# One signal for each corner of an item, in place of one for each unit, in a deformable convolution

## The chip, the cores and the metric

The kernel runs on one core of one Trainium2 chip. The metric is the time of one execution on the device in microseconds (us). The kernel before was timed three times.

## The reference

The input x has 4 images of 128 channels and 48 x 48 pixels, in float32. Two layers are computed, each added to its input:

```python
x = x + deform_conv_bn_relu(group_norm(x))   # layer 0
x = x + conv3x3(group_norm(x)) + bias        # layer 1

# layer 0, for each pixel and each of the 9 taps:
om   = conv3x3(x, w_offset) + b_offset       # 27 channels: dy, dx, mask
cols = mask * (corner(y0, x0)     * (1-ly)*(1-lx) + corner(y0, x0+1)     * (1-ly)*lx
             + corner(y0+1, x0)   * ly*(1-lx)     + corner(y0+1, x0+1)   * ly*lx)
out  = einsum('bckhw,ock->bohw', cols, wk) + b_conv
```

The four corners are gathered at places that depend on the data, and `out` then goes through a batch norm and a relu.

## The kernel before, in words

The 4 x 2304 pixels are cut into 24 **chunks** of 384 pixels (3 tiles of 128). A **unit** is one tap for one tile: 128 pixels on the partitions, 4 corners of 128 channels each in the free direction of tile `g`. A chunk has 9 taps x 3 tiles = 27 units, grouped into 9 **items** of 3 units (one tap, three tiles). The first and the last chunk order their units by tile; the last chunk has 11 items, and its two last ones have 2 and 1 units.

Layer 0 is a pipeline over items, written out by hand on five queues; semaphores tie them together:

- POOL issues one indirect DMA for each unit (line 299), 27 for a chunk, which fetches all four corners from a table in DRAM into `g`. It starts on a chunk when the chunk's indices are ready (`idx_ready`), and each group of three waits until the item of the chunk before that used its place in `g` is summed (`lerped`, line 297). `g` has one place for each unit, so chunk c+1 is fetched while the later items of chunk c are still summed.
- ACT multiplies the first corner by its weight, one instruction for each unit, into PSUM tile `PA` (line 557; semaphore `scaled`). It copies transposed items out of PSUM (`cols`, line 538; waits for `turned` and `conved`, signals `copied`), and copies a finished chunk out (`o`, line 548).
- DVE adds the products of corners 1, 2 and 3 (line 770): for an item of three units, nine instructions, corner by corner and in each corner unit by unit. Corners 1 and 2 write back into `PA`, corner 3 writes `acc`. Each one signals `lerped`. An instruction of corner 2 or 3 waits for the instruction of the corner before on the same unit. After item 4 of a chunk DVE computes the indices of the next chunk (lines 708 to 744; `idx` is line 717), and after item 2 the statistics of the chunk before (line 754).
- PE transposes `acc` (line 403; waits for `lerped`, signals `turned`), multiplies by the weights (line 392; signals `conved`), and spreads the offset convolution of the next chunk over items 0, 1 and 2 (line 352).
- The order on ACT is: scale item k, copy item k-1, and for k = 1 copy out the chunk before. So ACT can't scale item 2 of a chunk before it has copied item 0 and the chunk before.

After the 24 chunks come the batch norm, the relu and layer 1, which the change doesn't touch.

Of the kernel before, what the change touches and what calls it, by code (L numbers as in the profile page):

```python
# [6 lines left out]
ALU = mybir.AluOpType  # L7
ACT = mybir.ActivationFunctionType

P = 128  # L10
B, H, W = 4, 48, 48
HW = H * W
TAPS = 9
PW = W + 2
TILES = 3
# [20 lines left out]
LAST_SETS = ((0, 1, 2), (3, 4, 5), (6, 7), (8,))  # L36

TILE_ROWS = 3
LERP = 3


def items(c):

    if c not in BY_TILE:
        return [[(k, t) for t in range(TILES)] for k in range(TAPS)]
    return [[(k, t) for k in taps] for t in range(TILES) for taps in (LAST_SETS if (c, t) == (ALL - 1, TILES - 1) else TAP_SETS)]


def first_item(c):
    return sum(len(items(i)) for i in range(c))  # L50


def units_before(c, i):

    return c * TAPS * TILES + sum(len(units) for units in items(c)[:i])


def last_use(c, unit):
# [32 lines left out]
def build(nc, x_d, tab_d, woff_d, wconv_d, w1_d, boff_d, par_d, grid_d, out_d):  # L91

    with ExitStack() as ctx:
# [12 lines left out]
        g = sb("g", [P, TAPS, TILES, 4, P])  # L106

        mixed = g[:].rearrange("p k t q c -> p (k t q c)")[:, 0:MIX * PW * HALF].rearrange("p (m r w) -> p m r w", m=MIX, w=HALF)
        acc = sb("acc", [P, 3, TILES, P])
# [156 lines left out]
        @block.gpsimd  # L266
        def _(pl):
            xn4 = xn[:].rearrange("p (b r) w -> p b r w", b=B)
            pl.memset(wz[:], 0.0).then_inc(consts, 1)
            pl.memset(eps[:], EPS).then_inc(consts, 1)  # L270
            pl.memset(last_stats[:, 0:1], float(B * HW - 2 * P)).then_inc(consts, 1)
            pl.memset(gshift[:], 0.0).then_inc(consts, 1)
            pl.memset(gavg[:], 1.0 / GROUP).then_inc(consts, 1)
            pl.memset(ident[:], 0.0).then_inc(consts, 1)
            gv = gavg[:].rearrange("p (a b) -> p a b", b=GROUP)
            pl.wait_ge(consts, 5)
            pl.affine_select(out=gv, in_=gv, compare_op=ALU.is_ge, fill=0.0, base=0,
                             pattern=[[-GROUP, P // GROUP], [0, GROUP]], channel_multiplier=1).then_inc(consts, 1)
            pl.wait_ge(consts, 7)
            pl.affine_select(out=gv, in_=gv, compare_op=ALU.is_ge, fill=0.0, base=GROUP - 1,  # L280
                             pattern=[[GROUP, P // GROUP], [0, GROUP]], channel_multiplier=-1).then_inc(consts, 1)
            pl.affine_select(out=ident[:], in_=ident[:], compare_op=ALU.not_equal, fill=1.0, base=0,
                             pattern=[[-1, P]], channel_multiplier=1).then_inc(consts, 1)
            pl.memset(xn4[:, :, 0:PW:PW - 1, :], 0.0).then_inc(consts, 1)
            pl.memset(xn4[:, :, 1:1 + H, 0:PW:PW - 1], 0.0).then_inc(consts, 1)

            for c in range(ALL):
                pl.wait_ge(idx_ready, 1 if c == 0 else part_count(c))
                for i, units in enumerate(items(c)):
                    if c == 0 and i == len(TAP_SETS):  # L290
                        pl.wait_ge(idx_ready, 2)
                    if c:

                        used = max(last_use(c - 1, unit) for unit in units)
                        if i < len(items(c - 1)):
                            used = max(used, i)
                        pl.wait_ge(lerped, units_before(c - 1, used + 1) * LERP)
                    for k, t in units:
                        pl.indirect_dma_start(  # L299
                            out=g[:, k, t].rearrange("p q c -> p (q c)"), out_offset=None, in_=tab_d,  # L300
                            in_offset=bass.IndirectOffsetOnAxis(ap=idx[:, c % 2, t, k:k + 1], axis=0),
                        ).then_inc(gathered[i], 16)

            def add(b):
                for j in range(0, BANDS, 2):
                    pl.wait_ge(relued, b * BANDS + (BAND_ORDER.index(j) + 1))
                    add_band(pl, b, j).then_inc(added, 1)

            def mix_band(b, h):
                pl.wait_ge(normed, b * BANDS + (h + 1))  # L310
                if b:

                    pl.wait_ge(conv1, MIX * ((b - 1) * BANDS + min(h + 2, BANDS)))
                for m in range(MIX):
                    mix(pl, b, h, m).then_inc(mixed_ready, 1)

            add(0)
            for b in range(B - 1):
                mix_band(b, 1)
                mix_band(b, 2)  # L320
                add(b + 1)
                mix_band(b, 3)
                mix_band(b + 1, 0)
            for h in range(1, BANDS):
                mix_band(B - 1, h)

        @block.tensor
        def _(pe):
# [67 lines left out]
            def turn_item(c, i):  # L396
                units = items(c)[i]
                s = first_item(c) + i
                pe.wait_ge(lerped, units_before(c, i + 1) * LERP)
                if s > 1:  # L400
                    pe.wait_ge(copied, s - 1)
                for n in range(len(units)):
                    last = nc.tensor.transpose(TP[s % 2][:, n * P:(n + 1) * P], acc[:, s % 3, n, :], ident[:])  # L403
                last.then_inc(turned, 1)
# [87 lines left out]
        def _(act):  # L492
# [57 lines left out]
            def scale_item(c, i):  # L550
                s = first_item(c) + i
                act.wait_ge(gathered[i], landed(c, i))
                if s > 1:

                    act.wait_ge(lerped, (units_before(c, i - 1) if i else units_before(c - 1, len(items(c - 1)) - 1)) * LERP)
                for n, (k, t) in enumerate(items(c)[i]):
                    nc.scalar.activation(PA[s % 2][:, n * P:(n + 1) * P], g[:, k, t, 0, :], ACT.Copy,  # L557
                                         scale=wt[:, c % 2, 0, t, k:k + 1]).then_inc(scaled, 1)

            for i in (1, 3):  # L560
                act.dma_start(x[:, X0[i] * CP:X0[i + 1] * CP], x_d[:, 0, X0[i] * CP:X0[i + 1] * CP]).then_inc(x0_in[i], 16)
# [73 lines left out]
        def _(dve):  # L635
# [120 lines left out]
            def lerp_item(c, i):  # L756
                units = items(c)[i]
                s = first_item(c) + i
                done = units_before(c, i)
                dve.wait_ge(gathered[i], landed(c, i))  # L760

                dve.wait_ge(scaled, done + len(units))
                for q in range(1, 4):
                    for n, (k, t) in enumerate(units):
                        if q > 1:
                            dve.wait_ge(lerped, done * LERP + (q - 2) * len(units) + n + 1)
                        if q == 3 and n == 0 and s > 2:
                            dve.wait_ge(turned, s - 2)
                        a = PA[s % 2][:, n * P:(n + 1) * P]
                        nc.vector.scalar_tensor_tensor(acc[:, s % 3, n, :] if q == 3 else a, g[:, k, t, q, :],  # L770
                                                       wt[:, c % 2, q, t, k:k + 1], a, ALU.mult, ALU.add).then_inc(lerped, 1)

            statistics(0)
            deviation(0)
# [151 lines left out]
```

## Time and profile before

| | us |
|---|---|
| median of 3 runs | 1330.88 |
| lowest and highest | 1327.02 and 1339.39 |
| the profiled execution, its own time | 1331.31 |
| its span (first to last instruction) | 1329.6 |
| DVE busy | 687.7 (52% of the span) |
| POOL busy | 669.0 (50%) |
| PE busy (matmuls) | 783.9 (59%) |
| ACT busy | 369.8 (28%) |

Busy time is summed over each engine's instructions; waits and signals are not in it. No engine is busy for much more than half of the span, so the time is a matter of what waits for what. "Remote" or "issue" as the end of an idle time means that the profile names no instruction that ended just then.

### The profile page before, as it was taken

Reading aid. Unit: us, or ns where it says so; the run is one execution under the profiler, and the core shown is the slowest. Engines: PE = TensorE matmul, PEld = TensorE weight load, DVE = VectorE, ACT = ScalarE, POOL = GpSimd, SP = SyncE. Lnnn points to the kernel's source line nnn. Section 1 sums busy time; section 2 is a strip of 40 time slices with the busy share of each in tenths; the row PEclk is TensorE's granted clock in tenths of the full one; section 3 lists DMA queues with packets and bytes.
Section 4 is the critical chain, followed back from the end, with each engine's and each line's share of the span. In section 5 each row is a group of like instructions: output and inputs, shape, how many; then the busy total and the mean of one; then the engine's idle time right before and its main releaser. Section 6 shows DMA issues by size and latency. Waiting matters only on the chain.

```text
span 1329.6 us, 10583 instructions
## 1 busy us (share of the span) xinstructions
PE 783.9 (59%) x2380; PEld 376.8 (28%) x2380; DVE 687.7 (52%) x2662; ACT 369.8 (28%) x1026; POOL 669.0 (50%) x731
## 2 busy tenths in 40 slices
PE   7463646655555544656555544656555556555999
PEld 4232222222122222222122122222122122135777
DVE  4337446446447446446437536536436436465664
ACT  3213224223213214313213214313213213234320
POOL 4374374373473474374464465364364364361743
PEclk8665766767766767767776767767777677666999
DMA  7364464363473374373474364374364364360011
GB/s 282 118 183 126 118 199 117 111 201 108 119 206 108 116 209 117 104 208 108 116 204 114 117 197 129 99 199 120 104 203 123 107 198 127 104 176 22 37 53 54
DMA packets 55971, 181.50 MB, mean 137 GB/s; under 512 B 10980, under 2 KB 11492, under 8 KB 55524
## 3 DMA queue, kind: packets, MB, share of 16 engines
q0 software_dynamic: 51840, 169.91, 44.4%
q1 hardware_dynamic: 3780, 10.32, 2.1%
q10 hardware_dynamic: 288, 0.59, 0.1%
q14 instruction: 43, 0.35, 0.1%
q8 instruction: 20, 0.33, 0.1%
HBM read 176.06 MB, written 4.72 MB: 136 GB/s over the span
## 4 chain that ended last, share of the span: by engine, by line
another core or an unknown queue 27%; PE 22%; issue 21%; DVE 19%; ACT 10%; DMA 1%; POOL 1%; ACTq 0%; DVEq 0%; SPq 0%
DVE PA L770 10%; ACT PA L557 8%; PE OMT L352 5%; PE CO L392 5%; DVE acc L770 5%; PE TP L403 4%; PE TP L477 2%; PE PA L477 2%; PE CO L477 2%; ACT cols L538 1%; PE OMT L477 1%; PE VU L477 1%; DMA g<-corner_table,idx 1%; DVE bst L688 1%
## 5 line engine op out<-in xcount | busy, mean ns | idle before, releaser
L299 POOL DMA_INDIRECT g<-corner_table,idx x648 | 612.7, 946 | 581.4 <-DVE idx L717 366.2
L770 DVE SCALAR_TENSOR_TENSOR PA<-g,wt,PA 128x128 f32<-128x128 f32 x1296 | 358.0, 349 | 496.4 <-ACT PA L557 300.0
L403 PE MATMUL TP<-ident,acc 128*128 128x128 f32 x648 | 157.4, 367 | 398.4 <-DVE acc L770 216.8
L392 PE MATMUL CO<-cols,wcs 128*128 128x384 f32 (+1 forms) x504 | 266.1, 637 | 130.0 <-issue 100.1
L538 ACT ACTIVATE cols<-TP 128x384 f32<-128x384 f32 (+1 forms) x217 | 104.9, 484 | 736.8 <-remote 364.3
L403 PEld LDWEIGHTS TP<-ident,acc 128*128 128x128 f32 x648 | 90.2, 178 | 533.7 <-DVE acc L770 280.7
L352 PE MATMUL OMT<-xn,woff 128*27 128x384 f32 (+2 forms) x450 | 231.0, 671 | 1.2 <-ACT mask L519 0.7
L770 DVE SCALAR_TENSOR_TENSOR acc<-g,wt,PA 128x128 f32<-128x128 f32 x648 | 191.5, 342 | 63.5 <-DVE acc L770 36.5
L557 ACT ACTIVATE PA<-g,wt 128x128 f32<-128x128 f32 x648 | 203.3, 358 | 9.8 <-DMA g<-corner_table,idx 8.9
L392 PEld LDWEIGHTS CO<-cols,wcs 128*128 128x128 f32 x504 | 109.8, 279 | 160.1 <-issue 113.6
L352 PEld LDWEIGHTS OMT<-xn,woff 128*27 128x27 f32 x450 | 55.7, 138 | 177.7 <-issue 174.9
L245 POOL TENSOR_TENSOR g<-xn 128x288 f32<-128x288 f32 (+1 forms) x60 | 41.9, 731 | 34.3 <-ACT xn L623 33.2
L378 PE MATMUL CO<-vt,ut 9*128 9x384 f32 (+1 forms) x56 | 32.2, 666 | 0.0
L237 POOL TENSOR_TENSOR x<-x,o 128x576 f32<-128x576 f32 x8 | 11.5, 1454 | 23.1 <-ACT o L617 23.0
L530 ACT ACTIVATE vt<-VU 9x384 f32<-9x384 f32 x24 | 11.5, 478 | 32.4 <-issue 15.1
L367 PE MATMUL VU<-ident,vsum 128*9 128x128 f32 x72 | 17.7, 374 | 2.6 <-issue 2.6
L523 ACT ACTIVATE std<-OMT,eps 128x1 f32<-128x1 f32 x5 | 1.3, 261 | 59.4 <-PE OMT L335 59.4
L519 ACT ACTIVATE mask<-OMT 128x27 f32<-128x27 f32 (+2 forms) x25 | 4.8, 192 | 46.0 <-DVE pos L709 43.2
L548 ACT ACTIVATE o<-CO,params 128x384 f32<-128x384 f32 x23 | 13.2, 575 | 13.2 <-remote 12.8
L477 PE MATMUL OMT<-g,w 128*128 128x288 f32 x48 | 14.6, 444 | 2.2 <-DVE g L245 2.2
L496 ACT ACTIVATE xn<-x,gshift,gscale 128x1872 f32<-128x1872 f32 (+3 forms) x9 | 10.8, 1236 | 17.8 <-DVE gshift L682 11.1
L367 PEld LDWEIGHTS VU<-ident,vsum 128*9 128x9 f32 x72 | 9.1, 128 | 20.1 <-issue 18.6
(119 smaller groups left out, 495.7 us busy)
## 6 DMA issues: line engine op xcount, KB each, us to landing
g<-corner_table,idx POOLq DMA_INDIRECT x648
out_dram<-x SPq DMA_DIRECT2D x16, 288.0 KB, 2.1
x<-x_dram SPq DMA_DIRECT2D x3, 1152.0 KB, 8.1
wconv<-wconv_dram SPq DMA_DIRECT2D x1, 576.0 KB, 5.2
w<-w_dram SPq DMA_DIRECT2D x1, 576.0 KB
x<-x_dram ACTq DMA_DIRECT2D x1, 384.0 KB, 5.0
x<-x_dram SPq DMA_DIRECT2D x1, 384.0 KB, 4.7
x<-x_dram ACTq DMA_DIRECT2D x1, 192.0 KB, 3.5
```

Of the source, the lines that this page charges most:

```text
L245: return eng.tensor_tensor(mixed[:, m, first:first + rows, :], p, q, op)
L299: pl.indirect_dma_start(out=g[:, k, t].rearrange("p q c -> p (q c)"), out_offset=None, in_=tab_d, in_offset=bass.IndirectOffsetOnAxis(ap=i ...
L352: last = nc.tensor.matmul(OM[:, first * W:(first + rows) * W], woff[:, k, :], xn[:, row + k // 3:row + k // 3 + rows, k % 3:k % 3 + W], st ...
L367: last = nc.tensor.transpose(VT[:, t * P:(t + 1) * P], vsum[:, t, :], ident[:])
L378: nc.tensor.matmul(co_bank(c, t)[:, lo:hi], ut[:, c // CHUNKS % 2, :], vt[:, lo:hi], start=True, stop=False)
L392: last = nc.tensor.matmul(co_bank(c, t)[:, t * P:t * P + size], wcs[:, c // CHUNKS % 2, k, :], cols[:, s % 2, n * P:n * P + size], start=F ...
L403: last = nc.tensor.transpose(TP[s % 2][:, n * P:(n + 1) * P], acc[:, s % 3, n, :], ident[:])
L477: last = nc.tensor.matmul(MX[h % 2][m][:, 0:HB], w, mixed[:, m, r:r + BR, :], start=(ky == 0), stop=(ky == 2))
L538: nc.scalar.activation(cols[:, s % 2, 0:size], TP[s % 2][:, 0:size], ACT.Copy).then_inc(copied, 1)
L557: nc.scalar.activation(PA[s % 2][:, n * P:(n + 1) * P], g[:, k, t, 0, :], ACT.Copy, scale=wt[:, c % 2, 0, t, k:k + 1]).then_inc(scaled, 1)
L688: nc.vector.bn_stats(bst[:, j, :], x[:, b * HW + j * CP:b * HW + (j + 1) * CP]).then_inc(stats_in, 1)
L770: nc.vector.scalar_tensor_tensor(acc[:, s % 3, n, :] if q == 3 else a, g[:, k, t, q, :], wt[:, c % 2, q, t, k:k + 1], a, ALU.mult, ALU.add ...
```

## The change

DVE and ACT do the same instructions in the same order. What changes is which of them signal, and what is waited for:

- ACT's three scalings of an item signal `scaled` once, from the last one, in place of three times.
- DVE's three sums of one corner signal `lerped` once, from the last one: 3 signals for an item in place of 9.
- The wait of corner 2 and corner 3 stands once, ahead of the first unit, and is for the whole corner before. Before, each unit waited for its own unit alone.
- The counts that POOL, PE and ACT wait for are rewritten to match. They stand for the same moments: a whole item done.

```diff
--- before.py
+++ after.py
@@ -36,6 +36,7 @@
 LAST_SETS = ((0, 1, 2), (3, 4, 5), (6, 7), (8,))
 
 TILE_ROWS = 3
+
 LERP = 3
 
 
@@ -48,11 +49,6 @@
 
 def first_item(c):
     return sum(len(items(i)) for i in range(c))
-
-
-def units_before(c, i):
-
-    return c * TAPS * TILES + sum(len(units) for units in items(c)[:i])
 
 
 def last_use(c, unit):
@@ -294,7 +290,7 @@
                         used = max(last_use(c - 1, unit) for unit in units)
                         if i < len(items(c - 1)):
                             used = max(used, i)
-                        pl.wait_ge(lerped, units_before(c - 1, used + 1) * LERP)
+                        pl.wait_ge(lerped, (first_item(c - 1) + used + 1) * LERP)
                     for k, t in units:
                         pl.indirect_dma_start(
                             out=g[:, k, t].rearrange("p q c -> p (q c)"), out_offset=None, in_=tab_d,
@@ -396,7 +392,7 @@
             def turn_item(c, i):
                 units = items(c)[i]
                 s = first_item(c) + i
-                pe.wait_ge(lerped, units_before(c, i + 1) * LERP)
+                pe.wait_ge(lerped, (s + 1) * LERP)
                 if s > 1:
                     pe.wait_ge(copied, s - 1)
                 for n in range(len(units)):
@@ -552,10 +548,10 @@
                 act.wait_ge(gathered[i], landed(c, i))
                 if s > 1:
 
-                    act.wait_ge(lerped, (units_before(c, i - 1) if i else units_before(c - 1, len(items(c - 1)) - 1)) * LERP)
+                    act.wait_ge(lerped, (s - 1) * LERP)
                 for n, (k, t) in enumerate(items(c)[i]):
-                    nc.scalar.activation(PA[s % 2][:, n * P:(n + 1) * P], g[:, k, t, 0, :], ACT.Copy,
-                                         scale=wt[:, c % 2, 0, t, k:k + 1]).then_inc(scaled, 1)
+                    last = nc.scalar.activation(PA[s % 2][:, n * P:(n + 1) * P], g[:, k, t, 0, :], ACT.Copy, scale=wt[:, c % 2, 0, t, k:k + 1])
+                last.then_inc(scaled, 1)
 
             for i in (1, 3):
                 act.dma_start(x[:, X0[i] * CP:X0[i + 1] * CP], x_d[:, 0, X0[i] * CP:X0[i + 1] * CP]).then_inc(x0_in[i], 16)
@@ -756,19 +752,19 @@
             def lerp_item(c, i):
                 units = items(c)[i]
                 s = first_item(c) + i
-                done = units_before(c, i)
                 dve.wait_ge(gathered[i], landed(c, i))
 
-                dve.wait_ge(scaled, done + len(units))
+                dve.wait_ge(scaled, s + 1)
                 for q in range(1, 4):
+                    if q > 1:
+                        dve.wait_ge(lerped, s * LERP + q - 1)
+                    if q == 3 and s > 2:
+                        dve.wait_ge(turned, s - 2)
                     for n, (k, t) in enumerate(units):
-                        if q > 1:
-                            dve.wait_ge(lerped, done * LERP + (q - 2) * len(units) + n + 1)
-                        if q == 3 and n == 0 and s > 2:
-                            dve.wait_ge(turned, s - 2)
                         a = PA[s % 2][:, n * P:(n + 1) * P]
-                        nc.vector.scalar_tensor_tensor(acc[:, s % 3, n, :] if q == 3 else a, g[:, k, t, q, :],
-                                                       wt[:, c % 2, q, t, k:k + 1], a, ALU.mult, ALU.add).then_inc(lerped, 1)
+                        last = nc.vector.scalar_tensor_tensor(acc[:, s % 3, n, :] if q == 3 else a, g[:, k, t, q, :],
+                                                              wt[:, c % 2, q, t, k:k + 1], a, ALU.mult, ALU.add)
+                    last.then_inc(lerped, 1)
 
             statistics(0)
             deviation(0)
```

On DVE in a chunk of the middle, items 3 and 4, before (the line number of the sum is 770 before and 765 after, since lines went from the file; `gathered3` is the landing of item 3's gathers):

```order
L770 SCALAR_TENSOR_TENSOR PA<-g,wt,PA 128x128 [waits scaled,gathered3]
L770 SCALAR_TENSOR_TENSOR PA<-g,wt,PA 128x128 x2
L770 SCALAR_TENSOR_TENSOR PA<-g,wt,PA 128x128 [waits lerped] x3
L770 SCALAR_TENSOR_TENSOR acc<-g,wt,PA 128x128 [waits turned,lerped]
L770 SCALAR_TENSOR_TENSOR acc<-g,wt,PA 128x128 [waits lerped] x2
L770 SCALAR_TENSOR_TENSOR PA<-g,wt,PA 128x128 [waits scaled,gathered4]
L770 SCALAR_TENSOR_TENSOR PA<-g,wt,PA 128x128 x2
L770 SCALAR_TENSOR_TENSOR PA<-g,wt,PA 128x128 [waits lerped] x3
L770 SCALAR_TENSOR_TENSOR acc<-g,wt,PA 128x128 [waits turned,lerped]
```

and now:

```order
L765 SCALAR_TENSOR_TENSOR PA<-g,wt,PA 128x128 [waits scaled,gathered3]
L765 SCALAR_TENSOR_TENSOR PA<-g,wt,PA 128x128 x2
L765 SCALAR_TENSOR_TENSOR PA<-g,wt,PA 128x128 [waits lerped]
L765 SCALAR_TENSOR_TENSOR PA<-g,wt,PA 128x128 x2
L765 SCALAR_TENSOR_TENSOR acc<-g,wt,PA 128x128 [waits turned,lerped]
L765 SCALAR_TENSOR_TENSOR acc<-g,wt,PA 128x128 x2
L765 SCALAR_TENSOR_TENSOR PA<-g,wt,PA 128x128 [waits scaled,gathered4]
L765 SCALAR_TENSOR_TENSOR PA<-g,wt,PA 128x128 x2
L765 SCALAR_TENSOR_TENSOR PA<-g,wt,PA 128x128 [waits lerped]
L765 SCALAR_TENSOR_TENSOR PA<-g,wt,PA 128x128 x2
L765 SCALAR_TENSOR_TENSOR acc<-g,wt,PA 128x128 [waits turned,lerped]
```

The order is the same. Where all three sums of corner 2 and corner 3 waited, the first one waits now, and for the last sum of the corner before, which stands directly ahead of it.

On DVE at the end of the last chunk, the items of two units and of one unit, before:

```order
L770 SCALAR_TENSOR_TENSOR PA<-g,wt,PA 128x128 [waits scaled,gathered8]
L770 SCALAR_TENSOR_TENSOR PA<-g,wt,PA 128x128
L770 SCALAR_TENSOR_TENSOR PA<-g,wt,PA 128x128 [waits lerped] x2
L770 SCALAR_TENSOR_TENSOR acc<-g,wt,PA 128x128 [waits turned,lerped]
L770 SCALAR_TENSOR_TENSOR acc<-g,wt,PA 128x128 [waits lerped]
L770 SCALAR_TENSOR_TENSOR PA<-g,wt,PA 128x128 [waits scaled,gathered9]
L770 SCALAR_TENSOR_TENSOR PA<-g,wt,PA 128x128 [waits lerped]
L770 SCALAR_TENSOR_TENSOR acc<-g,wt,PA 128x128 [waits turned,lerped]
```

and now:

```order
L765 SCALAR_TENSOR_TENSOR PA<-g,wt,PA 128x128 [waits scaled,gathered8]
L765 SCALAR_TENSOR_TENSOR PA<-g,wt,PA 128x128
L765 SCALAR_TENSOR_TENSOR PA<-g,wt,PA 128x128 [waits lerped]
L765 SCALAR_TENSOR_TENSOR PA<-g,wt,PA 128x128
L765 SCALAR_TENSOR_TENSOR acc<-g,wt,PA 128x128 [waits turned,lerped]
L765 SCALAR_TENSOR_TENSOR acc<-g,wt,PA 128x128
L765 SCALAR_TENSOR_TENSOR PA<-g,wt,PA 128x128 [waits scaled,gathered9]
L765 SCALAR_TENSOR_TENSOR PA<-g,wt,PA 128x128 [waits lerped]
L765 SCALAR_TENSOR_TENSOR acc<-g,wt,PA 128x128 [waits turned,lerped]
```

In the item of one unit nothing differs: there the wait was already for the instruction directly ahead.

## Rows read from the trace of the kernel before

**Rows 1.** Page of the kernel before, costliest groups of instructions.

```profile
L299 POOL DMA_INDIRECT g<-corner_table,idx x648 | 612.7, 946 | 581.4 <-DVE idx L717 366.2
L770 DVE SCALAR_TENSOR_TENSOR PA<-g,wt,PA 128x128 f32<-128x128 f32 x1296 | 358.0, 349 | 496.4 <-ACT PA L557 300.0
L770 DVE SCALAR_TENSOR_TENSOR acc<-g,wt,PA 128x128 f32<-128x128 f32 x648 | 191.5, 342 | 63.5 <-DVE acc L770 36.5
```

**Rows 2.** Timeline of POOL, chunks 9 to 11: start, length, and idle time before.

```profile
463.35 0.94 POOL L299 DMA_INDIRECT g<-corner_table,idx  x1 [15.29 <-DVE idx L717]
...
511.89 0.94 POOL L299 DMA_INDIRECT g<-corner_table,idx  x1 [15.14 <-DVE idx L717]
...
544.40 0.95 POOL L299 DMA_INDIRECT g<-corner_table,idx  x1 [0.30 <-issue]
...
562.69 0.94 POOL L299 DMA_INDIRECT g<-corner_table,idx  x1 [17.34 <-DVE idx L717]
```

**Rows 3.** Windows by stage of chunk 10.

```profile
core 0: us, PE busy (x) PEld busy (x) DVE busy (x) ACT busy (x) POOL busy (x), PEclk, DMA share, GB/s
511.90:529.00 17.10, 7.68 (x20) 3.69 (x18) 11.03 (x52) 7.43 (x18) 13.14 (x14) 0.53 0.67 187
529.00:547.00 18.00, 5.10 (x12) 1.75 (x12) 5.63 (x20) 2.42 (x8) 12.39 (x14) 0.66 0.73 211
...
550.00:562.70 12.70, 12.44 (x54) 5.52 (x52) 9.85 (x41) 7.18 (x20) 0.01 (x1) 0.92 0.01 2
```

**Rows 4.** Timeline of DVE, items 0 and 1 of chunk 10.

```profile
531.14 0.87 DVE L770 SCALAR_TENSOR_TENSOR PA<-g,wt,PA 128x128 f32<-128x128 f32 x3
536.46 0.35 DVE L770 SCALAR_TENSOR_TENSOR PA<-g,wt,PA 128x128 f32<-128x128 f32 x1 [4.46 <-remote]
537.86 0.35 DVE L770 SCALAR_TENSOR_TENSOR PA<-g,wt,PA 128x128 f32<-128x128 f32 x1 [1.05 <-DVE PA L770]
...
548.37 0.35 DVE L770 SCALAR_TENSOR_TENSOR PA<-g,wt,PA 128x128 f32<-128x128 f32 x1 [4.47 <-remote]
```

**Rows 5.** Timeline of all engines, chunk 1.

```profile
69.03 0.94 POOL L299 DMA_INDIRECT g<-corner_table,idx  x1 [19.26 <-DVE PA L770]
...
85.04 0.55 PE L403 MATMUL TP<-ident,acc 128*128 128x128 f32 x3
...
92.22 0.49 ACT L538 ACTIVATE cols<-TP 128x384 f32<-128x384 f32 x1 [12.24 <-remote]
...
105.52 0.58 ACT L548 ACTIVATE o<-CO,params 128x384 f32<-128x384 f32 x1 [12.81 <-remote]
...
107.01 0.49 ACT L538 ACTIVATE cols<-TP 128x384 f32<-128x384 f32 x1
107.04 1.39 DVE L770 SCALAR_TENSOR_TENSOR PA<-g,wt,PA 128x128 f32<-128x128 f32 x5 [24.55 <-ACT PA L557]
```

**Rows 6.** Timeline of POOL, ACT, DVE and PE, chunk 18.

```profile
909.95 0.94 POOL L299 DMA_INDIRECT g<-corner_table,idx  x1 [16.21 <-DVE idx L717]
...
947.92 0.49 ACT L538 ACTIVATE cols<-TP 128x384 f32<-128x384 f32 x1 [10.68 <-remote]
...
949.82 1.65 DVE L770 SCALAR_TENSOR_TENSOR PA<-g,wt,PA 128x128 f32<-128x128 f32 x6 [8.66 <-ACT PA L557]
...
954.01 0.87 PE L403 MATMUL TP<-ident,acc 128*128 128x128 f32 x3
...
956.79 1.65 DVE L770 SCALAR_TENSOR_TENSOR PA<-g,wt,PA 128x128 f32<-128x128 f32 x6 [1.78 <-ACT PA L557]
```

**Rows 7.** Timeline of DVE, items 3 and 4 of chunk 9.

```profile
506.11 1.63 DVE L770 SCALAR_TENSOR_TENSOR PA<-g,wt,PA 128x128 f32<-128x128 f32 x6
...
508.42 1.64 DVE L770 SCALAR_TENSOR_TENSOR PA<-g,wt,PA 128x128 f32<-128x128 f32 x6
```

**Rows 8.** Timeline of DVE, last item of the last chunk (one unit).

```profile
1213.12 0.74 DVE L770 SCALAR_TENSOR_TENSOR PA<-g,wt,PA 128x128 f32<-128x128 f32 x2
1213.89 0.35 DVE L770 SCALAR_TENSOR_TENSOR acc<-g,wt,PA 128x128 f32<-128x128 f32 x1
```

## Prediction

> **What bounds the kernel now.** I read the page's groups first, then POOL's timeline, then the windows of one chunk, then the waits on DVE and ACT inside it. No engine is full, but POOL shows the beat: it issues 648 gathers and sits idle 581.4 us before them, 366.2 us of that until DVE's index instruction [rows 1]. In chunk 10 the first gather starts at 511.89 and the last at 544.40, 26 steps of 1.25 us, and then POOL waits until 562.69, when the indices of chunk 11 are there [rows 2]. Chunks 1 to 10 took (562.69 - 69.03) / 10 = 49.4 us each [rows 2, 5]. So a chunk is some 34 us of issue and some 15 us from the last gather to the next indices, and all that DVE does in these 15 us is on the path.
>
> The windows show why DVE is not done by then. While gathers are issued and land, DMA moves 187 to 211 GB/s, and in the second half of that DVE is busy for 5.63 of 18 us; when they are over it is busy for 9.85 of 12.70 us [rows 3]. Between, DVE's sums stand 1.40 us apart, and once 4.46 us behind the sum before, where three sums in a row otherwise take 0.87 us [rows 4]. Signals arrive late there. A signal of PE shows it more plainly: in chunk 1 PE has transposed item 0 by 85.6 us, and ACT, which has nothing else to do, goes on at 92.22, at 105.52 and at 107.01 [rows 5]. Then all signals that were under way are there at once. This clearing comes at the same distance from the first gather: 107.01 - 69.03 = 38.0 us in chunk 1, 947.92 - 909.95 = 38.0 in chunk 18 [rows 5, 6]. In chunk 18 DVE starts item 2 at 949.82, 1.9 us after it, since ACT first copies item 0 and the finished chunk and scales item 2 [rows 6].
>
> The period is thus: 38.0 us to the clearing, 1.9 us of ACT, then items 2, 3 and 4 and the indices on DVE, 9 to 11 us.
>
> **Part 1: signals that go (6 of 9 on DVE, 2 of 3 on ACT).** They take no busy time. Where they are late they cost: 1.40 us for each on DVE in items 0 and 1 of a chunk. But does the clearing come sooner with fewer of them? Chunk 1 is the test: DVE is idle for 24.55 us before its sum at 107.04 [rows 5], so no signal of DVE's can be in the way for most of that time, and the clearing is at 38.0 us all the same as in chunk 18. PE's signals, which keep their number, are late there too. So the clearing belongs to the gathers. What items 0 and 1 gain ends in a longer wait for item 2, and I take zero. The exceptions are chunks 4, 10 and 16, where item 0 starts late and item 1 runs over the clearing: in chunk 10 DVE starts the second corner of item 1 at 548.37 [rows 4], and PE, which does its work in order, is late for item 1 and all behind it. That chunk took 562.69 - 511.89 = 50.8 us against 48.5 of chunk 9 [rows 2]. With three signals for an item instead of nine, item 0 should end some microseconds sooner. The gain is between 0 and 2.3 us; PE's and ACT's extra work in these chunks stays, so I take 1.25 us, less the price of part 2: a net -1.0 us for each, **-3 us** for the three.
>
> The Trainium skill ("VectorE: DVE Perf Modes", section "The DRAIN you can't avoid") reports eight copies in a chain taking the same time with a signal from each and from the last alone. No run here shows that yet; it would leave only the late signals as a gain.
>
> **Part 2: the wait that gets closer.** Before, the first unit of a corner waits for an instruction two places back; now for the one directly ahead. Three sums of 349 ns take 0.87 us [rows 1, 4], so they start (0.87 - 0.35) / 2 = 0.26 us apart: each starts before the one ahead has ended. With a wait for the one directly ahead this overlap is lost. The last item of the last chunk has one unit and so has this wait already: its sums start (1213.89 - 1213.12) / 2 = 0.385 us apart [rows 8]. The price is 0.385 - 0.26 = 0.125 us for each corner change, two in an item, **0.25 us for an item**. From below it is bounded by 0 (if the overlap were kept), from above by the 1.40 us of a late signal [rows 4]. After the clearing, where the path is, DMA is at rest and [rows 8] is the nearest row, so I take 0.125.
>
> How much of it is on the path:
> - Items 5 to 8, 0 and 1 run before the clearing, with idle time behind them. Zero, as long as item 1 ends before the clearing.
> - Items 2, 3 and 4 run after it. In 4 of the 22 middle chunks (3, 9, 14, 15) item 4 follows item 3 without a gap: chunk 9 has item 3 at 506.11 and item 4 at 508.42, 2.31 us, just nine sums [rows 7]. Three items count: 0.75 x 4 = 3.0 us.
> - In chunks 1 and 8 a gap of 0.17 us takes some of it: 0.58 x 2 = 1.2. In 6, 12 and 21 the gap is 0.4 to 0.5: 0.35 x 3 = 1.0. In 19 it takes all that items 2 and 3 add: 0.25.
> - In 9 more (2, 5, 7, 11, 13, 17, 18, 20, 22) item 4 waits for PE: in chunk 18 the transposes of item 2 start at 954.01, long after item 2, and item 4 at 956.79 after 1.78 us of idle time [rows 6]. What items 2 and 3 add is hidden there: 0.25 x 9 = 2.25.
> - Chunk 0 has two items on the path, 0.5. In the last chunk five items follow the clearing with two corner changes each, some of it under ACT's work: 1.1. There POOL also waits for items of chunk 22 in another order than they are summed, so that its gathers start later by what items 5 to 8 add: 1.0.
>
> Sum: 3.0 + 1.2 + 1.0 + 0.25 + 2.25 + 0.5 + 1.1 + 1.0 = 10.3, less 3 = **+7.3 us**.
>
> **Part 3: signals that are coarser.** PE, POOL and ACT waited for whole items already, and DVE for all three scalings, and the last instruction of each still signals. Zero, with nothing to hide.
>
> The profiled execution took 1331.31, 0.43 above the median. 1331.3 + 7.3 = 1338.6 against it, **1338** against the median, +0.5%.
>
> **Rivals.**
> 1. *The close wait meets late signals (slower).* Before, a sum's own signal had a quarter of a microsecond to arrive without holding anything; now none. If items 6 to 8 or 0 and 1 then pay 1.40 us at each of two corner changes, item 1 runs over the clearing in all chunks, as in chunk 10. Each of 19 chunks goes from 49.4 to 50.8: 27 us more, and the 10.3 of part 2: 1331 + 27 + 10 = **1368**. For it: the 4.46 us in [rows 4]. Against it: item 1 gets rid of six late signals at the same time. It decides where item 1 ends later than 38 us after the first gather.
> 2. *Fewer signals free the line (faster).* If PE's signals wait behind DVE's, item 2 could run ahead of the clearing in some 20 chunks. That saves what lies between the starts of items 2 and 3, nine sums and the statistics, 2.8 us: -56, +7: **1282**. Chunk 1 speaks against it; for it, that DVE's own signals do arrive slowly.
> 3. *The close wait costs nothing.* If instructions of DVE didn't overlap anyway, only the -3 us would be left: **1328**. The 0.26 us step against 0.349 us of duration speaks against it [rows 1, 4]. The same section of the Trainium skill says that a next operation doesn't start before the pipe is empty, which would give this result; the trace disagrees for these instructions.
>
> **How the numbers follow.** The forecast has 0.54, of which 0.08 lies above 1344 (a dearer corner change); rival 1 0.13, rival 2 0.15, rival 3 0.12, and 0.06 is for what I don't see, half on each side. The range goes from a little below rival 3 to rival 1, 1322 to 1368, and leaves out rival 2 and the unseen. One per cent, about what a measurement can tell from no change, is 1318 to 1344. Faster: 0.15 + 0.03 = 0.18. Slower: 0.08 + 0.13 + 0.03 = 0.24. Same: 0.58.
>
> **What the profile after would show.** Right: the clearing at 38.0 us after a chunk's first gather; nine sums after it in 2.67 us rather than 2.42; items 0 and 1 shorter and the idle time before item 2 longer; chunks 4, 10 and 16 no longer the longest. Wrong, if item 2 starts sooner than 39.9 us after the first gather (rival 2), if item 1 ends after 38 us in most chunks (rival 1), or if a corner change costs other than 0.125 us.

## The result, and the profile after

The changed kernel takes 1343.35 us (median of 10 runs, 1340.82 to 1348.47), the kernel before 1331.42 (10 runs, 1327.02 to 1339.39). The ratio is 1.0091 with a 95% interval of 1.0072 to 1.0109: slower by 12 us, a little under one per cent. The profiled execution of the changed kernel took 1343.5, its span is 1341.7.

From the page of the kernel after, the groups of the gathers and of the sums, with the columns of [rows 1]:

```profile
L295 POOL DMA_INDIRECT g<-corner_table,idx x648 | 612.8, 946 | 592.5 <-DVE idx L713 375.4
...
L765 DVE SCALAR_TENSOR_TENSOR PA<-g,wt,PA 128x128 f32<-128x128 f32 x1296 | 376.0, 351 | 458.6 <-issue 224.4
...
L765 DVE SCALAR_TENSOR_TENSOR acc<-g,wt,PA 128x128 f32<-128x128 f32 x648 | 186.9, 344 | 83.6 <-remote 63.6
```

The sums last as long as before, 351 and 344 ns against 349 and 342, and there are as many. What grew is the idle time of POOL before its gathers, from 581.4 to 592.5 us, 11.1 us, which is nearly the whole loss. The beat that POOL shows got longer.

POOL's timeline after: the first gather of chunk 1, the first and the last of chunk 10, the first of chunk 11, and the first of the last chunk, to be laid beside [rows 2] and the first of [rows 5]:

```profile
69.70 0.94 POOL L295 DMA_INDIRECT g<-corner_table,idx  x1 [20.09 <-DVE PA L765]
...
516.51 0.94 POOL L295 DMA_INDIRECT g<-corner_table,idx  x1 [15.90 <-DVE idx L713]
...
549.01 0.95 POOL L295 DMA_INDIRECT g<-corner_table,idx  x1 [0.30 <-issue]
...
568.96 0.94 POOL L295 DMA_INDIRECT g<-corner_table,idx  x1 [19.01 <-DVE idx L713]
...
1168.61 0.94 POOL L295 DMA_INDIRECT g<-corner_table,idx  x1 [15.79 <-DVE idx L713]
```

Before, the first gather of the last chunk stood here:

```profile
1158.56 0.94 POOL L299 DMA_INDIRECT g<-corner_table,idx  x1 [16.56 <-DVE idx L717]
```

Chunks 1 to 22 take (1168.61 - 69.70) / 22 = 49.95 us each, and took (1158.56 - 69.03) / 22 = 49.52. That is 0.43 us for a chunk and 9.4 us for 22. The rest is 0.7 us ahead of chunk 1 and 2.1 us in the last chunk (from its first gather to the start of its last sum 57.4 against 55.3 us). Within chunk 10 the gathers take what they took, 549.01 - 516.51 = 32.5 us; what follows is longer.

The price of a close wait shows in the last item, of one unit, and in item 2 of chunk 18. First the last item, against [rows 8]:

```profile
1225.27 0.74 DVE L765 SCALAR_TENSOR_TENSOR PA<-g,wt,PA 128x128 f32<-128x128 f32 x2
1226.05 0.35 DVE L765 SCALAR_TENSOR_TENSOR acc<-g,wt,PA 128x128 f32<-128x128 f32 x1
```

It has not changed, 0.39 us from sum to sum. Then chunk 18 (POOL's first gather, ACT's first copy after the clearing, DVE's items 2 and 3, PE's transposes of item 2, item 4), against [rows 6]:

```profile
918.61 0.94 POOL L295 DMA_INDIRECT g<-corner_table,idx  x1 [16.65 <-DVE idx L713]
...
956.67 0.49 ACT L534 ACTIVATE cols<-TP 128x384 f32<-128x384 f32 x1 [8.59 <-remote]
...
958.58 1.78 DVE L765 SCALAR_TENSOR_TENSOR PA<-g,wt,PA 128x128 f32<-128x128 f32 x6 [5.36 <-ACT PA L553]
960.39 0.86 DVE L765 SCALAR_TENSOR_TENSOR acc<-g,wt,PA 128x128 f32<-128x128 f32 x3
...
961.64 1.76 DVE L765 SCALAR_TENSOR_TENSOR PA<-g,wt,PA 128x128 f32<-128x128 f32 x6
...
962.77 0.81 PE L399 MATMUL TP<-ident,acc 128*128 128x128 f32 x3
...
965.50 1.78 DVE L765 SCALAR_TENSOR_TENSOR PA<-g,wt,PA 128x128 f32<-128x128 f32 x6 [1.19 <-ACT PA L553]
```

The clearing is 956.67 - 918.61 = 38.1 us after the first gather, where it was, and item 2 starts at 958.58 - 918.61 = 40.0. It lasts from 958.58 to 961.25, 2.67 us; nine sums took 2.41 before. Item 4 waits for PE as before: the transposes of item 2 start at 962.77, 1.5 us after the item's end, so that what items 2 and 3 gained in length is eaten by the gap ahead of item 4, 1.19 us now and 1.78 before.

The windows of chunk 10, against [rows 3]:

```profile
core 0: us, PE busy (x) PEld busy (x) DVE busy (x) ACT busy (x) POOL busy (x), PEclk, DMA share, GB/s
516.50:533.00 16.50, 6.06 (x18) 3.53 (x18) 11.09 (x49) 6.72 (x16) 12.53 (x14) 0.59 0.66 186
533.00:551.50 18.50, 6.43 (x13) 1.88 (x11) 5.90 (x21) 3.16 (x10) 12.99 (x14) 0.68 0.73 210
554.50:569.00 14.50, 13.98 (x58) 5.96 (x57) 11.04 (x42) 7.41 (x20) 0.04 (x1) 0.91 0.01 2
```

In the stretch after the gathers DVE is busy for 11.04 of 14.50 us, where it was 9.85 of 12.70. In the second half of the gathers (533.00 to 551.50; this part of a chunk, up to the clearing, is called the **late stretch** from here on) nothing is won, with two thirds of DVE's signals gone: DVE is busy for 5.90 of 18.50 us, and was for 5.63 of 18.00. The timeline of DVE there, item 0 and the first corner of item 1 of chunk 10, against [rows 4]:

```profile
538.43 0.86 DVE L765 SCALAR_TENSOR_TENSOR PA<-g,wt,PA 128x128 f32<-128x128 f32 x3
545.34 0.87 DVE L765 SCALAR_TENSOR_TENSOR PA<-g,wt,PA 128x128 f32<-128x128 f32 x3 [6.05 <-remote]
549.54 0.86 DVE L765 SCALAR_TENSOR_TENSOR acc<-g,wt,PA 128x128 f32<-128x128 f32 x3 [3.33 <-issue]
550.33 0.86 DVE L765 SCALAR_TENSOR_TENSOR PA<-g,wt,PA 128x128 f32<-128x128 f32 x3
```

The three sums of a corner now go together, but the corners stand 6.9 and 4.20 us apart. Item 0 lasts from 538.43 to 550.40, 12.0 us. With nine signals it was 12.0 us too (531.14 to 543.12).

The rows also say what is late there. The six sums from 549.54 on start 0.26 us apart, in the midst of the late stretch, so DVE starts at once what has nothing to wait for. The sum at 545.34 waits for the signal of the sum that ended at 539.30. The trace records when a semaphore is raised, and has this one at 545.32: the signal was on its way for 6.0 us. It is the signals that come late. This is where the prediction was wrong about a part, and the experiments went there.

### The profile page after: what moved, and what is told of

It reads as the page before. It is cut to its first block, busy times and chain, and to the rows that moved or that the text cites. A ratio compares the mean times of both kernels' runs of the same rounds, so it can differ in the third digit from the quotient of the medians.

```text
span 1341.7 us, 10583 instructions
## 1 busy us (share of the span) xinstructions
PE 790.9 (59%) x2380; PEld 378.3 (28%) x2380; DVE 717.7 (53%) x2662; ACT 370.0 (28%) x1026; POOL 669.1 (50%) x731
## 4 chain that ended last, share of the span: by engine, by line
another core or an unknown queue 28%; PE 23%; issue 20%; DVE 16%; ACT 10%; POOL 1%; DMA 1%; ACTq 0%; DVEq 0%; POOLq 0%
DVE PA L765 9%; ACT PA L553 7%; PE CO L388 6%; PE OMT L348 5%; DVE acc L765 4%; PE TP L399 4%; PE TP L473 2%; PE PA L473 2%; PE CO L473 2%; DMA g<-corner_table,idx 1%; POOL g L295 1%; ACT cols L534 1%; PE OMT L473 1%; PE VU L473 1%
## 5 line engine op out<-in xcount | busy, mean ns | idle before, releaser
L295 POOL DMA_INDIRECT g<-corner_table,idx x648 | 612.8, 946 | 592.5 <-DVE idx L713 375.4
L765 DVE SCALAR_TENSOR_TENSOR PA<-g,wt,PA 128x128 f32<-128x128 f32 x1296 | 376.0, 351 | 458.6 <-issue 224.4
L388 PE MATMUL CO<-cols,wcs 128*128 128x384 f32 (+1 forms) x504 | 270.7, 647 | 136.3 <-issue 103.2
L765 DVE SCALAR_TENSOR_TENSOR acc<-g,wt,PA 128x128 f32<-128x128 f32 x648 | 186.9, 344 | 83.6 <-remote 63.6
```

The lines of the kernel that those rows point to most:

```text
L295: pl.indirect_dma_start(out=g[:, k, t].rearrange("p q c -> p (q c)"), out_offset=None, in_=tab_d, in_offset=bass.IndirectOffsetOnAxis(ap=i ...
L388: last = nc.tensor.matmul(co_bank(c, t)[:, t * P:t * P + size], wcs[:, c // CHUNKS % 2, k, :], cols[:, s % 2, n * P:n * P + size], start=F ...
L765: last = nc.vector.scalar_tensor_tensor(acc[:, s % 3, n, :] if q == 3 else a, g[:, k, t, q, :], wt[:, c % 2, q, t, k:k + 1], a, ALU.mult, ...
```

## The experiments

A remark on comparing them. Each run stands beside runs of the kernel before on the same chip, and only ratios are compared, since chips differ: the kernel before took 1331 us in the runs above, 1344.5 and 1344.0 us on the two chips of most of the experiments, and 949.7 us on a third one. What differs there is told with the runs on it.

**ACT's part alone.** The three scalings of an item signal once; DVE as before.

```diff
-    nc.scalar.activation(PA[...], g[:, k, t, 0, :], ...).then_inc(scaled, 1)
+    last = nc.scalar.activation(PA[...], g[:, k, t, 0, :], ...)
+last.then_inc(scaled, 1)
...
-dve.wait_ge(scaled, done + len(units))
+dve.wait_ge(scaled, s + 1)
```

> The kernel before with ACT's part of the change alone: scaled is signalled once for an item, from its last scaling; DVE's nine signals and their far waits stay. Theory W (the close wait alone moves the time): 0 +- 3 us against before, the clearing at 38.0 us after a chunk's first gather, nine sums in 2.41 us after it. Theory S (signals on the way are what costs, each one saved is a gain): 48 of 216 signals of an average chunk's item work go, so some us faster, and item 0 of chunks 4, 10 and 16 shorter than 12.0 us.

Measured: ratio 0.9995 (0.9982 to 1.0008). ACT's part is worth nothing, either way. Item 0 of chunks 4 and 16 lasts 12.0 us as ever, that of chunk 10 12.7.

**The waits alone, with all signals kept.** This separates the two halves of DVE's part.

```diff
-if q > 1:
-    dve.wait_ge(lerped, done * LERP + (q - 2) * len(units) + n + 1)
+if q > 1 and n == 0:
+    dve.wait_ge(lerped, done * LERP + (q - 1) * len(units))
```

> The kernel before with its 9 signals for an item and 3 from ACT kept, but with the waits of the change: the first sum of corner 2 and 3 waits for all sums of the corner before. Theory W: the whole loss is here, +12 us (+0.9%), nine sums in 2.68 us. Theory S: slower than the changed kernel, because the close wait is paid and the late signals too: item 0 of chunks 4, 10 and 16 longer than 12.0 us, +12 to +20 us. Had the loss come from coarse signals instead of close waits: 0.

Measured: ratio 1.0100 (1.0074 to 1.0125). With its nine signals and the close waits the kernel loses what the change loses. Item 0 of chunks 4, 10 and 16 lasts 12.0 us, not longer: against the theory that signals cost.

**Fewer signals without a close wait.** Corners 1 and 2 signal twice, corner 3 once; the first sum of a corner waits for the last but one of the corner ahead.

```diff
-        a, ALU.mult, ALU.add).then_inc(lerped, 1)
+        a, ALU.mult, ALU.add)
+if n == len(units) - 1 or (q < 3 and n == len(units) - 2):
+    ins.then_inc(lerped, 1)
...
-if q > 1:
+if q > 1 and (n == 0 or n == len(units) - 1):
+    # n == 0: for the last but one; n == 2: for the last
```

> Fewer signals without a close wait: corners 1 and 2 signal from their last but one and their last unit, corner 3 from its last, so 5 signals for an item of three units in place of 9; the first sum of the next corner waits for the last but one. Theory W: 0 +- 3 us against before, nine sums in 2.41 us. Theory S: a gain that the changed kernel hid behind its close waits, -5 to -20 us, item 0 of chunks 4, 10 and 16 some us shorter than 12.0. Theory I (in the late stretch each instruction of DVE takes its turn, with or without a signal): item 0 there stays at 12.0 us as it did in the changed kernel.

Measured: ratio 1.0002 (0.9985 to 1.0018). Four of nine signals gone, nothing lost and nothing won. The timeline of DVE, item 0 of chunk 10:

```profile
542.13 0.86 DVE L781 SCALAR_TENSOR_TENSOR PA<-g,wt,PA 128x128 f32<-128x128 f32 x3
548.86 1.06 DVE L781 SCALAR_TENSOR_TENSOR PA<-g,wt,PA 128x128 f32<-128x128 f32 x3 [5.87 <-remote]
552.37 0.60 DVE L781 SCALAR_TENSOR_TENSOR acc<-g,wt,PA 128x128 f32<-128x128 f32 x2 [2.44 <-remote]
554.46 0.35 DVE L781 SCALAR_TENSOR_TENSOR acc<-g,wt,PA 128x128 f32<-128x128 f32 x1 [1.49 <-issue]
```

From 542.13 to 554.81 it is 12.7 us, and 11.9 and 12.0 in chunks 4 and 16. With 9, 5 and 3 signals the item takes 12 us. So a late stretch doesn't charge for signals.

**Indices one item sooner.** This was meant to test the picture of the period: 38 us to the clearing, and then the items until the indices.

```diff
 # PE (its old place, behind conv_item, is left out)
+if ahead and k == 3:
+    turn_offsets(part_count(c + 1) - 1)
 turn_item(c, k)
 # ACT (its old place, behind copy_cols, is left out)
 scale_item(c, k)
+if ahead and k == 4:
+    masks(part_count(c + 1) - 1)
 # DVE
-if c + 1 < ALL and k == 4:
+if c + 1 < ALL and k == 3:
     indices(c + 1, part_count(c + 1) - 1)
```

> The kernel before with the indices of the next chunk computed one item sooner (after item 3 of a chunk in place of item 4), PE's transpose of the offsets ahead of its transpose of item 3, and the mask ahead of the copy of item 3. This tests that the period of a chunk is 38.0 us to the clearing and then the items until the indices, and nothing else. If so, each of 22 chunks gets shorter by item 4 and its gap, 2.4 to 3.5 us: -50 to -75 us, 1255 to 1280. If the period is bound by POOL or DMA or by PE, the time stays.

Measured: ratio 1.0090 (1.0065 to 1.0116), slower, where -4 to -6% was expected. The timelines of POOL and DVE for chunk 10 (first gather; the starts of item 8 of chunk 9 and of items 0, 1, 2 and 3 of chunk 10; first gather of chunk 11):

```profile
520.90 0.95 POOL L299 DMA_INDIRECT g<-corner_table,idx  x1 [17.23 <-DVE idx L717]
...
539.94 0.87 DVE L770 SCALAR_TENSOR_TENSOR PA<-g,wt,PA 128x128 f32<-128x128 f32 x3 [2.00 <-issue]
...
550.13 0.87 DVE L770 SCALAR_TENSOR_TENSOR PA<-g,wt,PA 128x128 f32<-128x128 f32 x3
...
557.44 0.87 DVE L770 SCALAR_TENSOR_TENSOR PA<-g,wt,PA 128x128 f32<-128x128 f32 x3
...
561.88 1.65 DVE L770 SCALAR_TENSOR_TENSOR PA<-g,wt,PA 128x128 f32<-128x128 f32 x6 [1.11 <-ACT PA L557]
...
565.46 1.65 DVE L770 SCALAR_TENSOR_TENSOR PA<-g,wt,PA 128x128 f32<-128x128 f32 x6 [0.69 <-ACT PA L557]
...
571.24 0.94 POOL L299 DMA_INDIRECT g<-corner_table,idx  x1 [14.19 <-DVE idx L717]
```

The order did what it should: the indices come after item 3. But chunk 10 still takes 571.24 - 520.90 = 50.3 us. Item 8 of the chunk before now starts 19.0 us after the first gather, when the stretch is late already; before it was 16.6 (528.45 - 511.89). It then takes some 10 us itself (539.94 to 550.13), and item 0 starts at 29.2 us (19.2 before). In chunks 2 to 21 other than 4, 10 and 16 item 1 starts at 38.8 to 39.7 us, after the clearing, where it was item 2. There six items start between the first gather and the clearing and three after it, whichever they are. The item that was taken off one end of the period came back at the other. So the picture of the period holds in its times (38 us, then items) and was wrong in what decides which items come after: it is how many DVE gets through before.

**Close waits on either side of the clearing.** All signals kept, close waits in items 2 to 4 alone, or in all others.

```diff
-if q > 1:
+if q > 1 and 2 <= i <= 4:      # or: not 2 <= i <= 4
+    if n == 0:
+        dve.wait_ge(lerped, done * LERP + (q - 1) * len(units))
+elif q > 1:
     dve.wait_ge(lerped, done * LERP + (q - 2) * len(units) + n + 1)
```

> The kernel before with all its signals, and the close waits in items 2, 3 and 4 of each chunk alone, the ones that run after the clearing. The theory that a chunk's period is 38.0 us, 1.9 us of ACT, and the items after it gives most of the loss: 0.264 us for each of three items in the chunks without a gap, less where item 4 waits for PE, +6 to +12 us. Rival: a close wait costs wherever it stands, since items before the clearing also get later: then only 3 of 9 of it, +4 us.

> The kernel before with all its signals, and the close waits in items 5 to 8, 0 and 1 alone, the ones that run before the clearing. If the clearing sets item 2, what they add is hidden: 0 to +3 us. Rival: +8 us.

Both ran on the chip where the kernel before takes 949.7 us, and there they measured 0.9998 (0.9987 to 1.0008) and 1.0014 (1.0004 to 1.0024). The window of one chunk's time in the run with close waits in items 2 to 4:

```profile
core 0: us, PE busy (x) PEld busy (x) DVE busy (x) ACT busy (x) POOL busy (x), PEclk, DMA share, GB/s
355.00:389.00 34.00, 22.86 (x84) 10.15 (x84) 24.03 (x97) 17.83 (x47) 25.77 (x28) 0.80 0.72 212
```

POOL is busy for 25.77 of 34 us, which with its 0.30 us between two gathers is no break at all. Nor does POOL wait for indices at the border to chunk 11; the rows are two gathers at that border:

```profile
387.47 0.95 POOL L299 DMA_INDIRECT g<-corner_table,idx  x1 [0.30 <-issue]
388.73 0.94 POOL L299 DMA_INDIRECT g<-corner_table,idx  x1 [0.30 <-issue]
```

And DVE's item 0 of the chunk, in the midst of gathers:

```profile
367.30 1.64 DVE L773 SCALAR_TENSOR_TENSOR PA<-g,wt,PA 128x128 f32<-128x128 f32 x6
368.85 0.86 DVE L773 SCALAR_TENSOR_TENSOR acc<-g,wt,PA 128x128 f32<-128x128 f32 x3
```

It lasts from 367.30 to 369.71, 2.4 us, where it took 12.0. Nothing is late on this chip: in the run with the other close waits the trace records each of DVE's 1944 signals within 0.02 us of the end of its sum. A chunk takes the 33.8 us that its 27 gathers take to issue, and the indices are ready some 26 to 32 us after the first gather (read in the run with the other close waits). There the path has no item that a close wait could lengthen, and those in items 2 to 4 cost 0. The +1.6 us of the others (0.4 to 2.3 by the interval) is not placed. The expectation of a later run puts it into the last chunk, but from the first gather to the end of the last sum that chunk takes 39.0 us in both profiled executions.

The same two kernels again, on a chip with late stretches (the kernel before 1344.0 us):

> As the run of the same kernel before, close waits in items 2 to 4 alone with all signals kept. On a late chip the theory of the path gives most of the loss here, +6 to +12 us; the rival that a close wait costs wherever it stands gives +4. On a prompt chip: 0.

> Close waits in all other items, all signals kept. On a late chip 0 to +4 us, of which some 2 lie in the last chunk, whose items 5 to 10 run after the last gather. Rival: +8 us. On a prompt chip +1 to +2 us, as it had there.

Measured: items 2 to 4, 1.0070 (1.0052 to 1.0089), +9.4 us; all others, 1.0033 (1.0017 to 1.0050), +4.4 us. Three ninths of the close waits make two thirds of the loss. The two add up to 1.0103, and the changed kernel had 1.0106 on that chip. In the profiled execution with close waits in the other items the last chunk (it has ten items, not the eleven named above) takes 57.7 us from its first gather to the start of its last sum, some 2.2 more than with ACT's part alone or with close waits in items 2 to 4. So about half of that run's loss is the last chunk's, and about 2 us are left for all chunks before it.

**The change itself again.**

> The changed kernel itself once more, since the kernel before took 949.7 us on the chip of the last four runs, where signals arrive promptly, and 1331 to 1344 us on the others, where they arrive late while gathers are in flight. On a late chip: +0.9% as before. On a prompt chip POOL issues without a break (33.8 us for a chunk) and the indices are ready before it needs them, so DVE's close waits are hidden in the middle chunks; only what follows the last gather remains, 1 to 2 us: +0.1 to +0.2%.

Measured, on the same chip with late stretches: 1.0106 (1.0087 to 1.0125). It was not run on the chip without them.

**Instructions in place of signals.** Three short instructions more for each item that neither wait nor signal.

```diff
 for q in range(1, 4):
+    nc.vector.memset(spare[:, q:q + 1], 0.0)
     for n, (k, t) in enumerate(units):
```

> The kernel before with three short DVE instructions more for each item, one ahead of each corner, that write an unused tile and neither signal nor wait. If in the late stretch each instruction of DVE takes a turn, signalled or not, item 0 of chunks 4, 10 and 16 goes from 12.0 us to 12.0 x 12/9 = 16 us; if each signal takes a turn, it stays at 12.0 us. After the clearing three short instructions add 0.2 us to an item, which gives +6 to +12 us either way.

It first ran on the chip without late stretches: 0.9998 (0.9988 to 1.0009), nothing, and it could say nothing on the question. Again, on a chip that has them:

> Three short DVE instructions more for each item, without signal or wait. On a late chip, if each instruction of DVE takes a turn in the late stretch, signalled or not, item 0 of chunks 4, 10 and 16 goes from 12.0 us to 16 us; if each signal takes a turn, or neither, it stays at 12.0 us. On a prompt chip: 0, as it had there.

Measured: 1.0522 (1.0498 to 1.0545), +70 us. The timelines of POOL and DVE in chunk 7 (its first gather, then item 0 and the start of item 1):

```profile
386.46 0.94 POOL L300 DMA_INDIRECT g<-corner_table,idx  x1 [19.61 <-DVE idx L718]
...
403.81 0.35 DVE L772 SCALAR_TENSOR_TENSOR PA<-g,wt,PA 128x128 f32<-128x128 f32 x1
...
411.25 0.35 DVE L772 SCALAR_TENSOR_TENSOR PA<-g,wt,PA 128x128 f32<-128x128 f32 x1 [5.53 <-remote]
412.65 0.35 DVE L772 SCALAR_TENSOR_TENSOR PA<-g,wt,PA 128x128 f32<-128x128 f32 x1 [1.05 <-issue]
...
419.67 0.35 DVE L772 SCALAR_TENSOR_TENSOR acc<-g,wt,PA 128x128 f32<-128x128 f32 x1 [1.05 <-issue]
...
421.04 0.36 DVE L772 SCALAR_TENSOR_TENSOR PA<-g,wt,PA 128x128 f32<-128x128 f32 x1 [0.49 <-issue]
422.45 0.06 DVE L765 MEMSET spare<- 128x1 f32 x1 [1.06 <-issue]
```

Item 0 lasts from 403.81 to 420.02, 16.2 us, and 12.0 x 12/9 = 16.0: the time goes with the number of instructions, signalled or not, at 12.0 / 9 = 1.33 and 16.2 / 12 = 1.35 us for one. With it item 1 ends only at some 39.8 us after the first gather in most chunks, behind the clearing, item 2 starts at 40.5 to 42.8, and chunks 1 to 22 take 53.1 us each: these are the 70 us. (In chunks 4, 10 and 16, which the expectation named, item 8 of the chunk before now takes the late time, and item 0, started only at 29.9 us, takes about 5.) The last row is an instruction that waits for nothing, and it starts 1.06 us late. That is so in this run alone. Of the DVE instructions without a wait that start 18 to 37.5 us after the first gather of one of chunks 1 to 22, 91 of 110 start here more than 0.15 us after the one ahead has ended, but none of 48 in the kernel before and none of 150 in the changed kernel. So the late stretch does not hold DVE's instructions in general. What the kernels share is that the signals come back at the pace of the instructions. Why DVE itself is held as well with the short writes among the sums is not shown; more sums without signals were not tried, so this can be a matter of the write.

**Gathers at a slower pace.** A POOL instruction of 0.53 us behind each gather.

```diff
     ).then_inc(gathered[i], 16)
+    pl.wait_ge(paced, paces[0])
+    pl.affine_select(out=sv, in_=sv, ...).then_inc(paced, 1)
```

> The kernel before with one instruction of POOL of some 0.5 us behind each gather, so that gathers start about 1.75 us apart and not 1.25. The gathers of a chunk then take 47 us and not 34. If signals are late because of the pace at which gathers come, they are prompt now, the items run beside the gathers, and the period is 47 to 49 us: -3% to 0. If late signals belong to any gather in flight, the clearing moves to 52 us and the period to 62: +25%.

Measured, on the chip without late stretches: 1.2712 (1.2690 to 1.2735). POOL's timeline there:

```profile
241.12 0.95 POOL L304 DMA_INDIRECT g<-corner_table,idx  x1 [0.17 <-issue]
242.08 0.53 POOL L309 TENSOR_SCALAR_AFFINE_SELECT spare<-spare 128x128 f32<-128x128 f32 x1
242.78 0.95 POOL L304 DMA_INDIRECT g<-corner_table,idx  x1 [0.17 <-issue]
```

A gather comes every 1.65 us, 27 of them in 44.6, and a chunk takes 44.6 us: on this chip the kernel is bound by POOL's issue. The question it was made for, whether late stretches come from the pace of the gathers, is open, since this chip has none.

## Why the prediction came out as it did

The time measured lies in the forecast range, the sign is right and the size was too small: +7.3 us forecast, +12 us measured, 1338 against 1343.

*Part 2, the close wait: right.* 0.125 us for a corner change was forecast from the item of one unit, and an item got 0.26 us longer (2.41 to 2.67). The loss is all here: the waits alone give 1.0100. The sums of the stages came out too: 2.1 us in the last chunk (forecast 1.1 + 1.0), 0.7 ahead of chunk 1 (0.5), and in the 19 middle chunks other than 4, 10 and 16 some 8.3 us (7.7). Within these 19 the agreement is partly luck. The four chunks without a gap got 3.5 us longer (3.0) and chunks 1 and 8 1.9 us (1.2), but chunks 6, 12 and 21 got 4.8 us longer (1.0), and the nine in which item 4 waits for PE got 2.0 us shorter (2.25 longer). In chunks 7, 13 and 22 that gap was 1.4 to 1.5 us and is gone in the trace after, in 6, 12 and 21 it grew from 0.3 to 0.4 us to some 1.0 to 1.2. Such gaps change from one execution to another: between the two runs that lose nothing (ACT's part alone, five signals) the same chunk differs by up to 1.8 us. So one pair of traces bears the sum over the chunks, not the price of each. Items before the clearing may not be wholly free, as I had them: about 2 us of the loss with close waits in the others lies ahead of the last chunk.

*Part 1, the signals that go: wrong, and this is the step that failed.* I read 1.40 us for each signal on DVE from [rows 4] and took -3 us for chunks 4, 10 and 16. They took 50.8, 52.5 and 51.1 us against 50.9, 50.8 and 51.6, together +1.1. The 1.40 us go with the number of instructions and not of signals: item 0 takes 12.0 us there with 9, 5 and 3 signals, and 16.2 with three instructions more. Each sum signalled, so that the rows before could not tell the two apart. With fewer signals DVE waits some 4 us for one instead of three times 1.40. What the prediction said the profile would show did not come either: item 0 is not shorter, the idle time before item 2 is shorter and not longer (item 1 ends 33.8 us after the first gather on average, 32.9 before), and chunks 4, 10 and 16 are still the longest of the middle ones. This term makes some 4 of the 4.7 us by which the forecast was too low; its +1.1 is no more than traces differ by, for the three chunks take 155.7 us together with ACT's part alone and 154.5 with five signals.

*That the clearing doesn't move: right.* In chunks 2 to 22 ACT's first copy after it stands at 38.0 to 38.2 us with 9 and 3 signals, and on the chip of the first experiments at 38.1 to 38.5 with 9 and 5. Chunk 1 of the trace before, with an idle DVE, had said so. There the row at 85.04 in [rows 5] is the transposes of item 1, and those of item 0 stand ahead of it:

```profile
81.84 0.55 PE L403 MATMUL TP<-ident,acc 128*128 128x128 f32 x3
```

ACT's copies of the two are at 92.22 and 107.01, so PE's signals were 9.8 and 21.4 us on their way.

*The rivals.* Rival 1 (the close wait meets late signals) did not come: item 1 ends ahead of the clearing on average, and later than 38.0 us after the first gather in five of the middle chunks, as before. Rival 2 (fewer signals free the line) fell with the run with five signals. Rival 3 (the close wait costs nothing) fell with the waits alone; sums without a close wait start 0.26 us apart at 0.35 us each, and the overlap that it denied is what the close wait costs. The prediction took the sentence about the empty pipe alone from the Trainium skill; the same section ("VectorE: DVE Perf Modes", section "The DRAIN you can't avoid") adds that a next operation that isn't held starts earlier. The trace agrees with that: 0.26 us apart without a close wait, and 0.39 with one. The Trainium skill's sentence in that section that a signal from each costs no more than one from the last is borne out by 0.9995 (ACT's part) and 1.0002 (five signals).

*What is open.* What makes signals late in the late stretch, why they come back at the pace of the instructions, and why one chip has no late stretch, was not found. On the other chips it comes with gathers in flight, and the same gathers at the same pace of one in 1.25 us leave the signals alone on this one. The pace of the gathers was not tried on a chip where it matters.

## What to carry to other kernels

A signal on an instruction costs nothing that these runs could see, and a wait for the instruction directly ahead costs the overlap of the two, 0.13 us for sums of 128 columns. So keep dependent instructions at least one apart, and don't buy fewer signals with closer waits. When a trace shows waits that end late, don't take the spacing for a price of each signal: here fewer signals came back just as late. Ask what else the same rows have as many of, and vary that. An instruction nearby that waits for nothing tells whether the engine or the signals are late; look at it in the kernel in question, since an instruction put in for the test can change it.

Before work is moved off the end of a period, ask what it will be behind at the beginning of the next. And before a fraction of a per cent is chased, see whether the time is the kernel's or the chip's: here the bound itself was another on one of the chips.

## What the hardware showed that I had not expected

- The same kernel takes 1331 to 1344 us on some chips and 949.7 us on another. On the former, in the later part of a chunk's gathers and until some 38 us after the first one, an item of DVE takes 12.0 us with 9, 5 or 3 signals, a signal of a sum to the next sum took up to 6.0 us (chunk 10 of the changed kernel), and one of PE to ACT 21.4 us (chunk 1 of the kernel before). On the latter, an item amid the gathers takes 2.4 us, and DVE's signals 0.01 to 0.02 us.
- In the late stretch sums that wait for nothing start 0.26 us apart as elsewhere (six in a row from 549.54 in the changed kernel). With writes of 0.06 us put among them, such a write starts 1.06 us after the one ahead has ended.
- Three instructions of 0.06 us for each item cost 5.2% on a chip with late stretches and nothing on the chip without.
- On the chip without late stretches POOL issues a gather every 1.25 us without a break, and a chunk takes 27 times that.
